# Gelu statistics from fp16 high and low halves of the folded sums, taken in head 14 instead of head 12

## What is computed

```python
def layer_norm(x):
    mean = jnp.mean(x, axis=-1, keepdims=True)
    var = jnp.var(x, axis=-1, keepdims=True)
    return (x - mean) / jnp.sqrt(var + EPS)
...
def bitlinear(x, w):
    xn = layer_norm(x)
    x_hat = xn + jax.lax.stop_gradient(absmax_quant(xn) - xn)
    w_hat = w + jax.lax.stop_gradient(ternarize_weights(w) - w)
    return jnp.einsum('bsd,od->bso', x_hat, w_hat)
h = bitlinear(x, w_fc)
h = jax.nn.gelu(h, approximate=False)
return bitlinear(h, w_proj)
```

## Time and profile before

| | |
|---|---|
| median of 3 runs | 1130.27 us (1126.84 to 1131.26) |
| the profiled execution | 1130.04 us, span of the profile 1128.2 us |
| PE busy, of the span | 1064.8 us, 94% |
| DVE | 868.7 us, 77% |
| ACT | 811.8 us, 72% |
| POOL | 537.8 us, 48% |
| the chain that ended last | PE 83%, ACT 7%, DVE 6%, issue 3% |
| mean granted PE clock | 0.977 of full |

### The profile page before, as it was taken

How to read it: one execution, slowest core, us unless ns; L and a number is a source line. 1 busy time by engine, 2 the same in 40 slices (tenths; PEclk the granted TensorE clock), 3 DMA queues, 4 the chain that set the end, 5 groups by cost and what they waited for, 6 DMA issues and landing times.

```text
span 1128.2 us, 26331 instructions
## 1 busy us (share of the span) xinstructions
PE 1064.8 (94%) x9484; PEld 676.4 (60%) x9484; DVE 868.7 (77%) x1623; ACT 811.8 (72%) x1372; POOL 537.8 (48%) x358
## 2 busy tenths in 40 slices
PE   5667899999999999999999999999999999999888
PEld 1334555656666565766666576666656566666555
DVE  4689768788787878788787878878787887877646
ACT  4786675868768686877868686776858687684944
POOL 0622271744629083553809264471917446280703
PEclk8978899999999999999999999999999999999989
DMA  8811203121121313112131311103131210212100
GB/s 338 314 40 31 83 1 76 58 63 59 29 78 37 74 56 74 56 28 66 37 93 37 74 56 42 58 31 93 37 74 56 56 56 28 48 39 57 58 20 19
DMA packets 75517, 74.20 MB, mean 66 GB/s; under 512 B 6608, under 2 KB 56016, under 8 KB 74960
## 3 DMA queue, kind: packets, MB, share of 16 engines
q1 hardware_dynamic: 75472, 73.59, 22.0%
HBM read 39.89 MB, written 8.39 MB: 43 GB/s over the span
## 4 chain that ended last, share of the span: by engine, by line
PE 83%; ACT 7%; DVE 6%; issue 3%; DMA 0%; POOL 0%; SPq 0%; ACTq 0%; DVEq 0%
PE F L824 10%; PE F L825 10%; PE F L665 8%; PE F L667 8%; PE QB L633 3%; PE QB L634 3%; PE QB L635 3%; PE QA L633 3%; PE QA L634 3%; PE QA L635 3%; PE T L862 2%; PE SB L722 2%; PE SA L722 2%; PE PV L739 2%; PE PV L738 2%
## 5 line engine op out<-in xcount | busy, mean ns | idle before, releaser
L824 PE MATMUL F<-yT_hi,fc_t 128*128 128x256 f16 x1024 | 228.1, 274 | 0.0
L825 PE MATMUL F<-yT_lo,fc_t 128*128 128x256 f16 x1024 | 227.8, 274 | 0.0
L592 POOL TENSOR_TENSOR rqk<-ssq,half 128x16 f32<-128x16 f32 x64 | 187.1, 2924 | 71.9 <-DVE ssq L1303 71.9
L665 PE MATMUL F<-proj_t,hs 128*128 128x512 f16 x512 | 194.1, 379 | 0.0
L667 PE MATMUL F<-proj_t,hs 128*128 128x512 f16 x512 | 193.8, 378 | 0.0
L561 POOL TENSOR_TENSOR acc<-acc,hg 128x512 f32<-128x512 f32 x96 | 152.1, 1584 | 11.4 <-ACT hg L966 2.8
L1269 DVE SCALAR_TENSOR_TENSOR hs<-hg,g_inv,hs 128x512 f16<-128x512 f32 x128 | 111.0, 868 | 57.4 <-ACT hs L971 57.2
L966 ACT ACTIVATE hg<-F,g_fc 128x512 f32<-128x512 f32 x128 | 87.4, 682 | 52.6 <-PE F L825 51.1
L561 POOL TENSOR_TENSOR acc<-hg 128x512 f32<-128x512 f32 x16 | 20.3, 1270 | 212.6 <-DVE hs L1269 177.0
L568 POOL TENSOR_TENSOR acc<-acc,hq 128x512 f32<-128x512 f32 x90 | 114.4, 1271 | 15.0 <-ACT hq L1028 4.7
L555 POOL TENSOR_TENSOR rs<-var,half 128x1 f32<-128x1 f32 x32 | 17.7, 552 | 216.2 <-DVE var L1149 216.2
(11 more groups left out here) (205 smaller groups left out, 2740.2 us busy)
## 6 DMA issues: line engine op xcount, KB each, us to landing
stk<-qkT SPq DMA_DIRECT2D x128, 128.0 KB, 2.5
xtok<-in_x SPq DMA_DIRECT2D x17, 512.0 KB, 3.3
xT_sb<-in_xT SPq DMA_DIRECT2D x16, 512.0 KB, 3.3
stk<-qkT SPq DMA_DIRECT2D x128, 64.0 KB, 2.1
xres<-in_x SPq DMA_DIRECT2D x15, 512.0 KB, 3.2
out<-xres SPq DMA_DIRECT2D x15, 512.0 KB, 2.8
stk<-in_w_emb SPq DMA_DIRECT2D x4, 512.0 KB, 5.3
fc_t<-in_w_qkv SPq DMA_DIRECT2D x2, 1024.0 KB, 12.0
```

The costliest lines, as they stand in the source:

```text
L592: pool.tensor_tensor(rqk[:, n % 2, :], ssq[:, n % 2, :], half[:, :], ALU.pow).then_inc(rqk_r, 1)
L665: pe.matmul(FB[t][:, :], hs[:, 0, k // 2, col:col + P], proj_t[:, k, :], start=(k == 0), stop=False)
L824: pe.matmul(dst, w, yT_hi[:, k, :], start=(k == 0), stop=False)
L825: mm = pe.matmul(dst, w, yT_lo[:, k, :], start=False, stop=(k == KT - 1))
```

## The change

Instead of fp32 `accf` against a column of ones, the statistics now use two fp16 tensors. ACT writes `acc_hi`, the fp16 rounding of `accf` times a scale (1/gamma for the sums, 1/(256 gamma²) for the squares), DVE writes `acc_lo`, the scaled value less `acc_hi`. PE multiplies both by a constant fp16 column, `mean16`, that holds 1/F or 256/F, and adds them in PSUM. So mean and variance come out scaled by gamma, and the constants behind follow (`eps_s`, `g_both`; `c1` is now a copy). The places move too: the fold to head 10, the split to head 12, the products to head 14 behind piece 3, POOL's root to head 14, c1 and c2 to head 15; on POOL the sums of the squares are 1 in head 0, 4 before head 7 and 2 before head 10, where they were 0, 4 and 3.

```diff
 TURN_AT = {4: ("piece", 0), 6: ("heads", 0), 7: ("piece", 1), 8: ("rms", 0), 10: ("heads", 1),
-           11: ("piece", 2), 12: ("stats", 0), 13: ("piece", 3), 15: ("heads", 2)}
+           11: ("piece", 2), 13: ("piece", 3), 14: ("stats", 0), 15: ("heads", 2)}
-FOLD_AT, RMS_AT, RS2_AT, STAT_AT, OUT1_AT = 11, 3, 12, 14, 15
+FOLD_AT, RMS_AT, RS2_AT, STAT_AT, OUT1_AT = 10, 3, 14, 15, 15
+SPLIT_AT = 12
+SQ_DOWN = 256.0
-SUMS_BEFORE = {0: [("h", n) for n in range(1, UNITS)], 7: [("q", n) for n in range(1, 5)],
-               10: [("q", n) for n in range(5, 8)]}
+SUMS_BEFORE = {0: [("h", n) for n in range(1, UNITS)] + [("q", 1)], 7: [("q", n) for n in range(2, 6)],
+               10: [("q", n) for n in range(6, 8)]}
...
+            pool.memset(mean16[:, 0:1], 1.0 / F).then_inc(c_pool, 1)
+            pool.memset(mean16[:, 1:2], SQ_DOWN / F).then_inc(c_pool, 1)
...
-                        pe.wait_ge(fold_r, nth(ffn, 1, 1))
+                        pe.wait_ge(sumlo_r, nth(ffn, 2, 2))
                         open_turn(("stats", 0))
                         for s in range(2):
                             for t in range(TT):
-                                mm = pe.matmul(T[:, s * TT + t:s * TT + t + 1], accf[:, s, t * P:(t + 1) * P],
-                                               ones[:, 0:1], start=True, stop=True)
+                                dst, rows = T[:, s * TT + t:s * TT + t + 1], slice(t * P, (t + 1) * P)
+                                pe.matmul(dst, acc_hi[:, s, rows], mean16[:, s:s + 1], start=True, stop=False)
+                                mm = pe.matmul(dst, acc_lo[:, s, rows], mean16[:, s:s + 1], start=False, stop=True)
...
+                    if h == SPLIT_AT and ffn is not None:
+                        act.wait_ge(fold_r, nth(ffn, 1, 1))
+                        for s, scale in ((0, g_inv), (1, g_sq)):
+                            act.activation(acc_hi[:, s, :], accf[:, s, :], ACT.Identity, scale=scale[:, 0:1]
+                                           ).then_inc(sumhi_r, 1)
...
-                dve.scalar_tensor_tensor(g_both[:, :], gam[:, 0:1], -1.0, gam[:, 1:2], ALU.mult, ALU.mult
-                                         ).then_inc(s_gam, 1)
+                dve.tensor_scalar(g_both[:, :], gam[:, 1:2], -1.0, None, ALU.mult).then_inc(s_gam, 1)
+                dve.wait_ge(s_gam, 6)
+                dve.tensor_scalar(g_sq[:, :], g_inv[:, :], g_inv[:, 0:1], 1.0 / SQ_DOWN, ALU.mult, ALU.mult
+                                  ).then_inc(s_gam, 1)
+                dve.tensor_scalar(eps_s[:, :], g_inv[:, :], g_inv[:, 0:1], EPS, ALU.mult, ALU.mult).then_inc(s_gam, 1)
...
+                    if h == SPLIT_AT and ffn is not None:
+                        for s, scale in ((0, g_inv), (1, g_sq)):
+                            dve.wait_ge(sumhi_r, nth(ffn, 2, s + 1))
+                            if s == 0:
+                                dve.wait_ge(fold_r, nth(ffn, 1, 1))
+                            dve.scalar_tensor_tensor(acc_lo[:, s, :], accf[:, s, :], scale[:, 0:1], acc_hi[:, s, :],
+                                                     ALU.mult, ALU.subtract).then_inc(sumlo_r, 1)
...
-                        dve.tensor_scalar(c1[:, :], st[:, 0, :], g_inv[:, 0:1], None, ALU.mult).then_inc(c_r, 1)
+                        dve.tensor_copy(c1[:, :], st[:, 0, :]).then_inc(c_r, 1)
```

More of the change, by code:

```diff
@@ L236, in adaln_ffn_kernel @@
         g_both = sb("g_both", [P, 1])
+        g_sq = sb("g_sq", [P, 1])
+        eps_s = sb("eps_s", [P, 1])
+        mean16 = sb("mean16", [P, 2], F16)
         colsum = sb("colsum", [P, D])
@@ L276, in adaln_ffn_kernel @@
         accf = sb("accf", [P, 2, N])
+        acc_hi = sb("acc_hi", [P, 2, N], F16)
+        acc_lo = sb("acc_lo", [P, 2, N], F16)
         st = sb("st", [P, 2, TT])
@@ L384, in adaln_ffn_kernel @@
         fold_r = sem("fold_r")
+        sumhi_r = sem("sumhi_r")
+        sumlo_r = sem("sumlo_r")
         st2_r = sem("st2_r")
@@ L436, in nothing @@
             pass
-        C_POOL = 7
+        C_POOL = 9
         block = ctx.enter_context(nc.Block())
@@ L1043, in _ @@
             act.wait_ge(s_gk, 1)
-            run(act, iteration, lambda: qkv_weights((0, 1)), nothing, lambda: act.wait_ge(s_gam, 7))
+            run(act, iteration, lambda: qkv_weights((0, 1)), nothing, lambda: act.wait_ge(s_gam, 9))
         @block.vector
@@ L1114, in proj_magnitude @@
                 dve.reciprocal(g_inv[:, :], gam[:, 0:1]).then_inc(s_gam, 1)
-                dve.scalar_tensor_tensor(g_both[:, :], gam[:, 0:1], -1.0, gam[:, 1:2], ALU.mult, ALU.mult
-                                         ).then_inc(s_gam, 1)
+                dve.tensor_scalar(g_both[:, :], gam[:, 1:2], -1.0, None, ALU.mult).then_inc(s_gam, 1)
[3 more added lines that the diff above has]
+                dve.tensor_scalar(eps_s[:, :], g_inv[:, :], g_inv[:, 0:1], EPS, ALU.mult, ALU.mult).then_inc(s_gam, 1)
             def last_weights():
-                dve.wait_ge(s_gam, 7)
+                dve.wait_ge(s_gam, 9)
             def input_lo(b, k):
@@ L1332, in iteration @@
                             dve.wait_ge(c_r, nth(ffn - 1, 2, 2))
-                        dve.tensor_scalar(st[:, :, :].rearrange("p s t -> p (s t)"), T[:, 0:2 * TT], 1.0 / F, None,
-                                          ALU.mult).then_inc(unturned, 1)
+                        dve.tensor_copy(st[:, :, :].rearrange("p s t -> p (s t)"), T[:, 0:2 * TT]).then_inc(unturned, 1)
                         dve.wait_ge(unturned, turn(i, ("stats", 0)) + 1)
@@ L1337, in iteration @@
                         dve.wait_ge(st2_r, nth(ffn, 1, 1))
-                        dve.scalar_tensor_tensor(var2[:, :], st[:, 1, :], EPS, st2[:, :], ALU.add, ALU.subtract
+                        dve.scalar_tensor_tensor(var2[:, :], st[:, 1, :], eps_s[:, 0:1], st2[:, :], ALU.add, ALU.subtract
                                                  ).then_inc(var2_r, 1)
+                    if h == SPLIT_AT and ffn is not None:
[5 more added lines that the diff above has]
+                                                     ALU.mult, ALU.subtract).then_inc(sumlo_r, 1)
                     if h == FOLD_AT and ffn is not None:
```

## The result

The changed kernel takes 1135.57 us (median of 6 runs, 1133.88 to 1136.58), the kernel before beside it 1129.99 us (6 runs, 1126.84 to 1131.34). The ratio is 1.0053, with a 95% interval of 1.0034 to 1.0071: slower by some 5.6 us. The prediction was 1128.7 us, with 1119 to 1134 as its range. The profiled execution took 1136.37 us (span 1134.6).

The account below looks back on a forecast made before the run. PE was taken as the bound, busy 99.56 of 100 us. From 1130.04 us, 14 passes gave -1.5, pass 15 -0.8 and the tail +0.96: 1128.7 us, range 1119 to 1134.

Parts of the forecast that it names:

- Taken away, -1.33, and the new block: PE at the old statistics place loses 1.33 us a pass; eight fp16 matmuls at the new place cost 0.27.
- microcode case: PE's statistics block: about 62 ns per matmul where microcode decodes each, so 0.50 us; an estimate of +4.2 us in all.
- Rival C: PE's eight small matmuls each pay their weight load, 0.77 us for 0.20: 1136.7 us; chance 0.03.
- The split on ScalarE and DVE: After head 12: two 128x256 operations on ACT, 0.49 us each, cost nothing; two on DVE, 0.48 each, not covered.
- Rival B: DVE's split pair, with two SBUF operands, takes 0.4 us more each: 1139.9 us, at half about 1134; chance 0.13.
- The statistics moved to head 14: a wait of 0.86: PE waits 0.86 us a pass before the statistics until DVE has read piece 3 from the shared bank T.
- rival A: The bank wait before the statistics does not come: 1115.4 us, half gone about 1122; chance 0.20 together, 0.12 whole.
- Fold moved to head 10: "Cost nothing": DVE's fold and POOL's sums move earlier; rqk ends at 561.30 against 561.56, qkn starts at 561.34 instead of 561.60.
- The end of the pass, 0.09 late: c1 and c2, about 0.3 us behind p_lo of head 15, put the last o_sb at 569.26; 0.11 us gain left.
- Pass 15, -0.8, and the tail, +0.96: Last pass, without bank wait, 0.8 us shorter (bounds -2.6, +2.6); tail 0.96 longer (0 to +1.5), ACT and DVE in series.
- signs of being wrong: Wait before the statistics under 0.4 us; or acc_lo over 0.6, or PE waiting over 0.3 for o_sb or v_lo at pass end.

Follow-up runs that it names:

- The order alone: Kernel before with the new tables (statistics in head 14, fold in head 10, new order of POOL's sums), fp32 product, no split: 1139.40 us.

## Why the prediction was wrong

By its own steps:

- **Taken away, -1.33, and the new block.** Right: A is -1.34, and the eight fp16 matmuls stand 0.025 apart, 0.21 in all for 0.27. The 25 ns that the Trainium skill gives ("TensorE: Matmul & The Clock Gate", section "Wait — 56ns, not 53.3ns?") hold here, and its microcode case does not. Rival C falls.
- **The split on ScalarE and DVE.** Right in size: acc_hi 0.50 and acc_lo 0.48, 0.39 apart. Rival B, as I put it (the pair at 0.8 us), did not happen.
- **The statistics moved to head 14: a wait of 0.86.** 0.88. But the reason that I gave was a third of it: I ascribed it to the chain on DVE. The order alone shows that 0.55 of it comes with the place, even with DVE idle. For the same reason rival A could not happen whole: ScalarE's half, which I had worked out and called "not the limit", keeps 0.60 of the wait.
- **Fold moved to head 10: "Cost nothing".** This step failed. It took rqk at the 2.92 of before; with the fold beside its start it is 3.29, qkn comes 0.37 later than worked out, and piece 3's turn waits 0.21 (B). (Only 0.17 of it was slack: of the 0.30 us between "ready at 562.02" and the turn at 562.32 go the 0.13 from an end on DVE to PE.) I had looked at the port only for the split's pair, where POOL was idle, and not for the fold, which has two SBUF operands of the same kind and had been moved to where POOL starts.
- **The end of the pass, 0.09 late.** This step failed in size: c1 and c2 took 0.38 for "about 0.3" and PE waits 0.23 (the sum itself used only 0.25: 567.79 and the 1.22 from oT_lo to o_sb make 569.01, and 0.3 more 569.31, not 569.26); and 0.13 of issue time that no row of before showed (E).
- **Pass 15, -0.8, and the tail, +0.96.** -0.47 and +0.77: right in sign, and small. The clock moved both. The stretch at half clock behind the last scores, for the earlier trace rows, came again (0.56 for 0.51), and ended sooner against the start of the tail, by 0.28 us. But pass 15 now has a second one (1.2 GHz) that the kernel before has not:

```profile
1064.30:1067.70 3.40, 3.40 (x40) 1.96 (x36) 1.49 (x3) 3.00 (x7) 2.56 (x3) 0.50 0.52 167
...
1086.80:1092.30 5.50, 5.50 (x16) 2.33 (x17) 1.09 (x3) 0.38 (x1) 0.00 (x0) 0.56 0.00 0
```

In front of it PE waited 2.33 us for a p_lo, and in the kernel before 2.34 at the same place, with the clock at full behind it. From the scores behind that wait to the P·V behind the next o_sb PE needs 7.11 us for 6.45; behind the o_sb after that, shorter waits have left 0.25 of the loss. How far this pass moves by itself show the two kernels with one DVE instruction more, which have the code of before in it and other stretches at half clock: 58.06 and 58.51 us for 57.25. So the -0.47 is within what pass 15 varies by, and its agreement in sign with the -0.8 settles nothing.

The sum per pass was -0.11 and came out at +0.38: 0.21 from rqk, 0.14 from o_sb, 0.13 from the issue, and 0.01 in all else. Fourteen passes make 6.9 us of it, as much as the whole miss. The range was too narrow for that: it took each of several steps 0.1 late (+0.3 a pass at most), while three were late at once, by 0.13 to 0.21 each. The sign hung on a gain of 1.33 and a new term of 1.13, both known to 0.02, and on three small steps, each of which had more room to be late than to be early. None of the prediction's signs of being wrong came: the wait was over 0.4, acc_lo under 0.6, and PE waited for o_sb by less than 0.3. They looked for one large error, and this was the sum of small ones.

## What to carry to other kernels

A step that is moved behind another user of the same bank pays that user's whole read-out (here 2.2 us, two engines in series) less what work lies between. Count it before counting what the step itself saves; and if PE is only waiting, put ready matmuls in front: that alone gained 0.53 us a pass, the cheaper product alone 0.13, and both together 1.08. When an instruction on DVE moves, look at what POOL starts in that moment, not only at what DVE had to do. And where a forecast is the difference of two large terms, the small steps decide its sign: give each its own bound to the late side.

## What I had not expected of the hardware

- DVE's fold, 0.68 us long, under way when POOL starts rqk: 3.29 us for 2.92. An SBUF sum of 1.01 us: 3.37; an SBUF copy of 0.75 us: 3.09. Each adds what is left of it when rqk starts, less 0.15 us. A fold that starts 1.3 us into rqk leaves both at their length.
- The first matmul of a pass starts 0.46 to 0.48 us behind the last turn of heads where the loop jumps back, and 0.22 where it does not. Behind a wait for o_sb both are longer, 0.59 to 0.65 and 0.27 to 0.36.
- The fp32 statistics block costs PE 0.91 us where PE has waited in front of it, behind P·V matmuls and in the tail behind matmuls of 512 columns alike, and 0.81 where it has not.
